# Two layers of graph attention on one core: value products of two units in one run, and four moves around it

## What is computed

```python
def layer0(x, adj):                       # x [128, 128, 256], adj [128, 128, 128]
    nx = ln(x) * g1 + b1
    q, k, v = heads(nx @ wq + bq), heads(nx @ wk + bk), heads(nx @ wv + bv)   # 8 heads of 32
    scores = q @ k.T / sqrt(32) + where(adj > 0, 0.1 * adj * adj, -inf)
    out = softmax(scores) @ v             # "value products"
    x1 = x + out @ wo + bo
    n2 = ln(x1) * g2 + b2
    return x1 + gelu(n2 @ w1 + b1) @ w2 + b2     # 256 -> 1024 -> 256
def layer1(x, adj):
    q, k, v = heads(x @ Wq + bq), heads(x @ Wk + bk), heads(x @ Wv + bv)
    scores = where(adj == 0, -inf, q @ k.T / sqrt(32))
    y = softmax(scores) @ v @ Wo + bo + x
    return ln(y) * gamma + beta
```

## Time and profile before

| | |
|---|---|
| median of 3 runs | 2196.47 us (2194.91 to 2199.86) |
| the profiled execution | 2196.19 us, span 2194.2 us |
| mean granted clock of TensorE | 0.989 |
| busy: PE, PEld | 98%, 85% |
| busy: DVE, ACT, POOL | 82%, 77%, 53% |
| DMA | 35 GB/s on the mean |

### The profile page before, as it was taken

How to read it: one execution, slowest core, us unless ns; L and a number is a source line. 1 busy time by engine, 2 the same in 40 slices (tenths; PEclk the granted TensorE clock), 3 DMA queues, 4 the chain that set the end, 5 groups by cost and what they waited for, 6 DMA issues and landing times.

```text
span 2194.2 us, 58906 instructions
## 1 busy us (share of the span) xinstructions
PE 2150.1 (98%) x20300; PEld 1859.1 (85%) x20300; DVE 1798.1 (82%) x8414; ACT 1682.3 (77%) x5646; POOL 1153.8 (53%) x1266
## 2 busy tenths in 40 slices
PE   7999999999999999999999999999999999999986
PEld 5788888888888888888888888888888888888875
DVE  6588888888888888888888888888888888888774
ACT  5578777778877778877787877787877787877773
POOL 4345655445655455555455555455555455554454
PEclk8899999999999999999999999999999999999998
DMA  4010111001111101111101111101110101110000
GB/s 128 25 32 31 40 33 36 27 29 37 37 35 31 32 28 37 34 39 31 32 26 40 33 40 30 30 28 40 33 40 27 33 28 40 33 40 26 26 14 17
DMA packets 94308, 75.74 MB, mean 35 GB/s; under 512 B 8128, under 2 KB 93760, under 8 KB 94016
## 3 DMA queue, kind: packets, MB, share of 16 engines
q1 hardware_dynamic: 94016, 71.99, 10.8%
HBM read 55.20 MB, written 16.78 MB: 33 GB/s over the span
## 4 chain that ended last, share of the span: by engine, by line
PE 96%; DVE 2%; issue 1%; ACT 1%; POOL 0%; DMA 0%; SPq 0%; POOLq 0%; ACTq 0%; DVEq 0%
PE p_bank L1132 67%; PE p_heads L1229 10%; PE p_heads L1216 8%; PE p_bank L1248 7%; PE p_bank L1151 4%; ACT scores L650 1%; DVE normed L885 0%; DVE probs_t L922 0%; DMA scores<-in_L_gnn_wk 0%; PE p_bank L1061 0%; PE p_bank L1087 0%; DVE scores L863 0%; ACT normed L661 0%; SPq L441 0%; DVE x_two L770 0%
## 5 line engine op out<-in xcount | busy, mean ns | idle before, releaser
L650 ACT ACTIVATE scores<-scores,negmax 128x128 f32<-128x128 f32 x2048 | 793.7, 392 | 22.5 <-DVE negmax L863 22.2
L584 POOL TENSOR_TENSOR scores<-scores,inverse 128x512 f32<-128x512 f32 x512 | 541.2, 1062 | 333.4 <-DVE inverse L874 333.4
L650 ACT ACTIVATION_READ_ACCUMULATOR scores<-scores,negmax 128x1 f32 x2048 | 391.9, 191 | 0.0
L1132 PEld LDWEIGHTS p_bank<-w_down,hidden 128*128 128x128 f32 x3072 | 374.7, 190 | 8.6 <-issue 5.9
L1132 PE MATMUL p_bank<-w_down,hidden 128*128 128x256 f32 x3072 | 381.9, 284 | 0.0
L1132 PE MATMUL p_bank<-normed,w_up 128*128 128x512 f32 x1536 | 370.5, 397 | 3.2 <-DVE normed L885 3.2
L1132 PEld LDWEIGHTS p_bank<-normed,w_up 128*128 128x128 f32 x1536 | 285.3, 189 | 68.9 <-issue 9.8
L1229 PE MATMUL p_heads<-ident,scores 128*128 128x128 f32 x2048 | 312.8, 276 | 9.2 <-issue 5.2
L863 DVE CUSTOM_DVE_ANT_0 scores<-p_heads,adj_a 128x128 f32<-128x128 f32 x1024 | 235.2, 286 | 44.4 <-issue 44.4
L673 ACT ACTIVATE p_bank<-p_bank,ready_cols 128x512 f32<-128x512 f32 x256 | 169.5, 662 | 132.8 <-PE p_bank L1132 127.1
L1229 PEld LDWEIGHTS p_heads<-ident,scores 128*128 128x128 f32 x2048 | 241.3, 141 | 35.3 <-DVE negmax L863 11.4
(11 more groups left out here) (117 smaller groups left out, 3698.0 us busy)
## 6 DMA issues: line engine op xcount, KB each, us to landing
res_a<-in_x SPq DMA_DIRECT2D x32, 512.0 KB, 3.8
out<-res_c SPq DMA_DIRECT2D x128, 128.0 KB, 1.7
x_in<-in_x SPq DMA_DIRECT2D x31, 512.0 KB, 3.8
adj_a<-in_adj SPq DMA_DIRECT2D x32, 256.0 KB, 2.9
adj_c<-in_adj SPq DMA_DIRECT2D x32, 256.0 KB, 2.8
piece_room<-in_L_gnn_w SPq DMA_DIRECT2D x2, 512.0 KB, 7.1
x_two<-in_x SPq DMA_DIRECT2D x1, 512.0 KB, 5.5
res_c<-in_L_gnn_w SPq DMA_DIRECT2D x1, 512.0 KB, 6.3
```

The source lines that it names most:

```text
L584: nc.gpsimd.tensor_tensor(rows_g, rows_g, inverse[:, step % 2, heads].unsqueeze(2).broadcast_to([P, HC, P]), ALU.mult).then_inc(probs_made, 1)
L650: last = nc.scalar.activation(scores[:, k % 2, h], scores[:, k % 2, h], ACT.Exp, scale=-1.0, bias=negmax[:, k % 2, h:h + 1], accum_out=tot ...
L1132: last = nc.tensor.matmul(dst, stationary(i), moving(j), start=(n == 0), stop=(n == total_n - 1))
```

## The change

Five things are changed.

1. The value products of two units stand in one run in steps 1, 3, 5 and 7, into one bank of 512 columns; `heads_high` and `heads_low` copy both units at once, and `probs_t` and `heads_t` have two rooms. The output products W stay one by one: the first of a pair in the step of the run, the second in the step after; in step 1 both. W of units C0 to C3 is thereby a step later than before, and so are their norm, `finish` and store. For stage M the norms of the last two units stand together in step 2.
2. Both V banks of stage A stand in the `early` place of step 2 (before: one `early`, one in `fill`).
3. On SP the load of `res_a` stands in front of store 1 instead of behind it.
4. On ACT the copies of a transposed block (`ahead`: XT M in step 2, XT N in step 7) stand in front of the second half of the exponentials, except in step 4.
5. At the start: bias products 7 and 2 are moved forward in pass 0; pieces 6 and 7 of the weights are split in steps 3 to 5 of pass 1 instead of 0 and 1; one `scaled_room` takes the place of two, with two more waits for it.

```diff
-HIGH_STEPS = {0: {1: [2], 4: [3], 5: [4], 6: [5]}, 1: {0: [6], 1: [7]}}
-LOW_STEPS = {0: {5: [3], 6: [4], 7: [5]}, 1: {0: [6], 1: [7]}}
+HIGH_STEPS = {0: {1: [2], 4: [3], 5: [4], 6: [5]}, 1: {3: [6, 7]}}
+LOW_STEPS = {0: {5: [3], 6: [4], 7: [5]}, 1: {4: [6], 5: [7]}}
...
+    by_step = {k: [] for k in steps}
     for r, k in enumerate(steps):
-        by_step[k] = ([("V", r - 2), ("W", r - 2)] if r >= 2 or pending else []) + (
-            [("T", r - 1)] if r >= 1 or pending else [])
+        by_step[k] += [("T", r - 1)] if r >= 1 or pending else []
+        by_step[k] += [("W", -3)] if r == 0 and pending else []
+        if r % 2 and (r >= 3 or pending):
+            by_step[k] += [("V", (r - 3, r - 2)), ("W", r - 3)]
+            if r == 1:
+                by_step[k] += [("W", r - 2)]
+            elif r < len(steps) - 1:
+                by_step[steps[r + 1]] += [("W", r - 2)]
     last = len(steps) - 1
-    tail = [("V", last - 1), ("T", last), ("W", last - 1), ("V", last), ("W", last)] if drain else []
+    tail = [("W", last - 2), ("V", (last - 1,)), ("T", last), ("W", last - 1), ("V", (last,)), ("W", last)] if drain else []
...
-        early = {1: ("Q", "A", 0), 2: ("V", "A", 0), 4: ("DOWN", 1), 6: ("Q", "C", 0), 7: ("V", "C", 0)}
+        early = {1: [("Q", "A", 0)], 2: [("V", "A", 0), ("V", "A", 1)], 4: [("DOWN", 1)], 6: [("Q", "C", 0)],
+                 7: [("V", "C", 0)]}
-        fill = {0: [("K", "A", 1)], 1: [("Q", "A", 1)], 2: [("V", "A", 1)],
+        fill = {0: [("K", "A", 1)], 1: [("Q", "A", 1)],
...
-            self.tail = self.tail[:-1] + [("V", "N", 0), self.tail[-1], ("V", "N", 1),
-                                          ("BIAS", 2), ("BIAS", 3), ("BIAS", 7)]
+            self.fill[7] = [("BIAS", 7)]
+            self.tail = self.tail[:1] + [("BIAS", 2)] + self.tail[1:-1] + [
+                ("V", "N", 0), self.tail[-1], ("V", "N", 1), ("BIAS", 3)]
...
-        probs_t = sb("probs_t", [P, H, P])
-        heads_t = sb("heads_t", [P, 2, KC, P], F32R)
+        probs_t = sb("probs_t", [P, 2, H, P])
+        heads_t = sb("heads_t", [P, 2, 2, KC, P], F32R)
-        scaled_rooms = [sb(f"scaled_room{i}", [P, 2, TOK]) for i in range(2)]
+        scaled_room = sb("scaled_room", [P, 2, TOK])
...
                 if s.c:
                     store(t, 0)
-                    store(t, 1)
                 if s.a and s.before is not None:
                     sp.wait_ge(*drained_use(t, ("DOWN", 1)))
                     sp.dma_start(res_a[:, :, :], x_view[:, bass.ds(t.group_a * GB, GB), :]).then_inc(res_a_loaded, 16)
                 if s.c:
+                    store(t, 1)
                     store(t, 2)
...
+                    for op in s.ahead.get(k, []) if not long else []:
+                        evacuate(t, op)
                     if k in s.units and k != s.behind and not long:
                         exps(t, k, 1)
-                    for op in s.ahead.get(k, []):
+                    for op in s.ahead.get(k, []) if long else []:
                         evacuate(t, op)
...
-                nc.scalar.activation(heads_t[:, HI].rearrange("p c n -> p (c n)"), p_bank[bank][:, 0:KC * P],
+                nc.scalar.activation(heads_part(HI, units), p_bank[bank][:, 0:len(units) * KC * P],
                                      ACT.Copy).then_inc(high_made, 1)
...
-                    if k == 2:
-                        for r in s.late.get(k, []):
-                            apply_norm(t, r, GB - 1)
+                    if k == 2 and s.m and s.pending:
+                        apply_norm(t, -1, 2)
+                        apply_norm(t, -1, 3)
...
+            def value_products(t, units):
+
+                bank, dst = take(t, ("O", units))
+                u_last, stage, _ = t.unit(units[-1])
+                pe.wait_ge(turned_out0, u_last + 1)
+                pe.wait_ge(turned_out1, u_last + 1)
...
+                for i, r in enumerate(units):
+                    _, _, b = t.unit(r)
+                    for h in range(H):
+
+                        j, c = h % HC, h // HC
+                        last = nc.tensor.matmul(dst[HD * j:HD * (j + 1), (i * KC + c) * P:(i * KC + c + 1) * P],
+                                                values[room(t, stage)][:, b, h * HD:(h + 1) * HD],
+                                                probs_t[:, parity(r), slot_of(c, j), :], start=True, stop=True)
+                last.then_inc(filled[bank], 1)
```

More of the change, by code:

```diff
@@ L88, in __init__ @@
         self.lag, self.tail = lags(self.steps, pending, drain)
-        self.late, waiting = {}, [-3] if pending else []
+        self.pending = pending
+        self.late, waiting = {}, []
         for k in self.steps:
@@ L137, in __init__, with use_units @@
         assert not self.looped or len(self.use) % BANKS == 0
+    def use_units(self, r):
+        return [use[1] for use in self.use if use[0] == "O" and use[1][0] == r]
     def number(self, ops):
@@ L330, in build @@
                                         piece_rooms[3][:, :, :])]
-        scaled = [as_piece(scaled_rooms[n % 2][:, :, :]) for n in range(8)]
+        scaled = [as_piece(scaled_room[:, :, :]) for n in range(8)]
         w1, w2 = w_view(L0 + "w1"), w_view(L0 + "w2")
@@ L410, in turned_columns, with parity, turned_rows, heads_part @@
             return p_heads[:, 2 * g:2 * g + 2, KC * P:2 * KC * P]
-        def turned_rows(g):
-            return probs_t[:, HC * g:HC * (g + 1)].rearrange("p (a h) n -> p a (h n)", a=2)
+        def parity(r):
+            return (r if r >= 0 else r + STEPS) % 2
+        def turned_rows(r, g):
+            return probs_t[:, parity(r), HC * g:HC * (g + 1)].rearrange("p (a h) n -> p a (h n)", a=2)
+        def heads_part(part, units):
+            first = parity(units[0])
+            return heads_t[:, part, first:first + len(units)].rearrange("p i c n -> p (i c n)")
         def room(t, what):
@@ L921, in turned, with heads_low @@
                 dve.wait_ge(probs_turned, u * KC + 2)
[L922 to L929, removed]
+                nc.vector.tensor_copy(turned_rows(r, 1), turned_columns(1)).then_inc(turned_out1, 1)
+            def heads_low(t, units):
+                bank, _ = t.bank(("O", units))
+                dve.wait_ge(high_made, t.high(("O", units)))
+                nc.vector.tensor_tensor(heads_part(LO, units), p_bank[bank][:, 0:len(units) * KC * P],
+                                        heads_part(HI, units).bitcast(F32), ALU.subtract).then_inc(drained[bank], 1)
             def add_residual(t, r):
@@ new lines, in project @@
+            def project(t, r):
+                for units in t.s.use_units(r):
+                    bank, number = t.bank(("O", units))
+                    pe.wait_ge(drained[bank], number)
+                bank, dst = take(t, ("W", r))
+                w = weight[weights_of[t.unit(r)[1]][3]]
+                three_passes(dst[:, 0:D], [(lambda i, c=c: heads_t[:, i, parity(r), c, :], lambda j, c=c: w[:, j, c, :])
+                                           for c in range(KC)]).then_inc(filled[bank], 1)
@@ L1235, in lagging @@
+            def lagging(t, op, which):
                 if op == "T":
                     for g in range(2):
-                        turn(t, r, g)
+                        turn(t, which, g)
                 if op == "V":
[L1239 to L1243, removed]
-                            pe.wait_ge(*drained_bank(*made(t, "V", stage, i)))
@@ L1245, in lagging @@
-                    for h in range(H):
-                        j, c = h % HC, h // HC
-                        last = nc.tensor.matmul(dst[HD * j:HD * (j + 1), c * P:(c + 1) * P],
-                                                values[room(t, stage)][:, b, h * HD:(h + 1) * HD], probs_t[:, slot_of(c, j), :],
-                                                start=True, stop=True)
-                    last.then_inc(filled[bank], 1)
-                if op == "W":
-                    bank, number = t.bank(("O", r))
-                    pe.wait_ge(drained[bank], number)
-                    bank, dst = take(t, ("W", r))
-                    w = weight[weights_of[stage][3]]
-                    three_passes(dst[:, 0:D], [(lambda i, c=c: heads_t[:, i, c, :], lambda j, c=c: w[:, j, c, :])
-                                               for c in range(KC)]
-                                 ).then_inc(filled[bank], 1)
+                    value_products(t, which)
```

28 lines of the change are left out of this document (14 added, 14 removed).

## The result

The changed kernel takes 2218.85 us (2217.77 to 2220.42), the kernel before 2196.47: ratio 1.0104, 95% interval 1.0093 to 1.0115. It is 1% slower, and the forecast of 2200 and its range up to 2217 were missed on the slow side. The profiled execution took 2218.9 us, span 2216.9, 22.7 more than the span before.

A forecast was written before the change was run, and what follows sets the result against it. PE's queue was taken to bound the loop. From 2196.2 us, 30 passes at +0.29 (+8.7), the start (-6.0) and the end (+1.5) gave 2200.4, forecast as 2200; own range 2190 to 2210, wider range 2178 to 2217.

The forecast's parts named there:

- wait in step 0: Step 0: PE waits for POOL's second probabilities behind finish of C3, biases, rstd and store; 0.64 us a pass.
- wait in step 6: Step 6, second transposes: PE comes 0.14 us earlier, POOL's row some 0.13 later; 0.15 us a pass (0 to 0.3).
- start, to pass 2: Passes 0 and 1: moved bias products and weight pieces gain 3.05, 1.3 and 2.7, less 1.0; net -6 us (-2 to -8).
- end, from pass 32 on: End: four units finished in one row instead of three, one finish (1.49) more; +1.5 us (0 to 4).
- V run: Value products of two units in one run on PE, four pairs a pass: saves 0.60 us a pass, 18 us in all.
- the 0.10 for the exponentials: Step 2: second exponentials come later behind the block's copies, delaying masks for step 3's transposes; 0.10 us a pass (0 to 0.25).
- 1 back: Pass 1: four weight copies ahead of step 4's exponentials, mostly under DOWN 1, and POOL's subtractions return 1 us of the start's gain.
- (b): Rival: DVE falls behind with doubled residuals, measurements and norms in steps 1 and 2, UP waits; 2215 to 2225 us, chance 0.14.
- upper bound in step 0: Step 0's stall at most 1.0 us a pass, if DVE's norm beside them stretches POOL's instructions.
- (a): Rival: POOL is not late, finish of C3 or its store ends sooner, PE keeps its gain; 2174 us (2168 to 2186), chance 0.18.
- (c): Rival: the wide copies end after W is due, each 0.1 us costing 0.4 a pass; 2212 us and up, chance 0.04.
- (d): Rival: the V run is not shorter, eight more products cost 0.57 us, stall about 0.75 a pass; 2214 us, chance 0.04.

The follow-up runs named there:

- e2: Changed kernel, with step 0's late probabilities on POOL ahead of store wait and res_c bias, and DVE's norm behind the copy of the turned probabilities: 2192.22 us, ratio 0.9983.
- f2: Changed kernel with e2, e4 and e7 together, and step 6's norm on DVE also behind its copy of the turned probabilities: 2178.42 us, ratio 0.9921.
- e6: Changed kernel, but ACT copies the blocks of steps 2 and 7 behind the second exponentials again, as before: 2235.26 us, ratio 1.0173.
- e3: Changed kernel, but C's finished blocks are written to and stored from a room of their own, so step 0's first res_c bias waits only for finish: 2211.53 us, 1.0066.
- e7: Changed kernel, but POOL's first res_a bias moves from step 5 into step 6, behind the probabilities of the second transposes: 2216.65 us, ratio 1.0088.
- e4: Changed kernel, but in pass 1 POOL scales weight piece 6 ahead of A's rstd in step 3 instead of behind it: 2215.81 us, ratio 1.0089.
- e9: Changed kernel without its start moves: bias products 2, 3, 7 at pass 0's end, weight pieces 6, 7 cut in steps 0, 1 of pass 1: 2222.98 us, 1.0122.
- e1: Changed kernel, but in step 0 POOL makes the late probabilities ahead of its wait for the store and the first res_c bias: 2238.85 us, ratio 1.0191.
- e8: Kernel before plus start moves alone: weight pieces 6, 7 cut in steps 3 to 5 of pass 1, bias products 7, 2 moved: 2199.84 us, ratio 1.0008.

## Why the prediction was wrong

The forecast by its terms, in us (left: as forecast; right: from the traces; the last two lines of the pass from e2 and f2):

```
                                   forecast   measured
pass with no wait, against before    -0.50      -0.49     (65.63 - 66.12; forecast: -0.60 + 0.10)
wait in step 0                       +0.64      +0.74     (5.97 - 5.23)
wait in step 6                       +0.15      +0.32     (5.54 - 5.22)
30 passes                            +8.7      +19.3      (30 x 0.57 = 17.1, late stores 2.2)
start, to pass 2                     -6.0       -3.05
end, from pass 32 on                 +1.5       +6.5
sum                                  +4.2      +22.7
```

The mechanism was right: the merged run pays on PE and POOL's row takes back more. The steps that failed are terms of the sum, each put too favourably. Of the 18.5 us between 4.2 and 22.7, the wait in step 6 has 5.1, the wait in step 0 3.0 and the late stores 2.2; the end has 5.0 and the start 3.0; the rest is rounding.

- **V run: right.** 1.01 us against 1.0; the steps without waits are 5.23 and 5.22 (forecast near 5.2) and 7.08 (near 7.1). That the whole line fits is partly luck: the 0.10 for the exponentials is not seen as such (the old order is worse, e6), steps 1 and 2 together came out 0.15 us longer than forecast, and step 5 0.14 shorter.
- **Step 0: the row was right, its spread was left out.** Counted from the start of step 7, the late probabilities were forecast to end at 10.9 us and end at 11.0. The forecast put the bias at the landing of the store, 0.07 us behind the rstd; e3 finds 0.15 us a pass for the store. But no room was left for stores that land later: the five late passes are 2.2 us.
- **Step 6: undersized by half.** I took PE to come 0.14 us earlier (+0.436 - 0.575). Step 5 grew by only 0.30, so PE came 0.27 earlier. And I looked at the transposes alone: DVE's copy behind them is next in line (e7, f2).
- **Start: "1 back" was 4.5.** Up to step 4 of pass 1 the -7.05 came (82.06 instead of 89.23 is 7.2). "1 back" for the copies in front of the exponentials was 3.6 in step 4 and 0.9 in step 5. I counted the four copies and hid them under DOWN 1; but they wait for POOL's scaling, which stands behind an rstd that DVE's sums for A release only when step 4 begins, and behind them the table load, the exponentials, their inverse, four norms, the mask and the addition for DOWN 1 follow one another through three engines. The 0.9 of step 5 goes with the clock: behind the wait of 3.53 us the granted clock is 0.50 from 92 to 96 us; in e4 and e9, without that wait, it is 1.00 in step 5, which takes 5.92 us.
- **The end: one row was carried over without its surroundings.** The finish of a fourth unit cost about what was forecast (2.0 us from the last scores on, against 1.5). What was left out is step 0 of pass 32, where the same POOL row waits 1.34 us for the store and PE stands 2.92 us. Behind it the granted clock is 0.58 and 0.50 in 2119 to 2122 and 2122 to 2126, and a V run takes 1.94 us instead of 1.08. The first three steps are 5.8 us longer than before; step 3 is 1.2 shorter. With the order of f2 pass 32 to the end is 99.2 us, +3.3; what makes up the rest was not tried.

Of the rivals, (b) names the time, 2215 to 2225, but not what happened: in the loop PE never waits for x_two; all three waits of that kind (5.9 us in sum) lie outside it. Its thought that DVE is close to the limit is right in another place, as e1 showed. The upper bound in step 0 had the pair of engines the wrong way round: it let DVE's norm stretch POOL's instructions, and it is POOL's that stretch the norm (last section). (a), (c) and (d) are out: POOL is late, heads_t is waited for only outside the loop (3.2 us in five waits), and the run is shorter. The residual's load ahead of a store and the single `scaled_room` were not tried alone; in the trace after no instruction waits for that load, as forecast.

## What to carry to other kernels

When an instruction moves into another step, write down the whole row of the engine that receives it, up to the next result that the bound engine needs, and then the same for the engine behind that: undoing the first link alone made this kernel slower (e1), both links made it faster than before (e2). A saving that is spread over a loop is kept only if the waits in it are moved with it: here a pass came out at +0.58 us, and with two reorders on POOL and two on DVE at -0.49. One-time work that is "hidden" must be followed back too: ask when its input is ready, not only what it runs under.

## What the runs showed of the hardware

**A norm on DVE that starts beside POOL waits for it.** The same form of instruction, 128x256 from SBUF to SBUF, lasts 0.40 to 0.41 us alone, but 1.36, 1.21 and 1.04 us in e1, e7 and e2, each time until 0.15 us after the end of a POOL bias (e1: 1060.01 and 1059.86; e7: 1038.46 and 1038.31). In the trace after, from 100 us on, all 180 norms that start while POOL works on an instruction of 256 or 512 columns end 0.15 to 0.28 us after it. A norm that starts 0.17 us ahead keeps its time (0.38 us at 1043.40), and POOL's probabilities beside it, at 1043.57, take 1.12 instead of 1.04. DVE's residual of the same size out of PSUM keeps its 0.41 to 0.43 inside a POOL bias. The Trainium skill, "SBUF — State Buffer", section "SBUF: two separate sides", says that a DVE instruction in a mode with two ports and a GpSimd instruction take one pair of ports as a lock, and the loser blocks; the traces agree, though no run shows in which mode the norm works. In the row that forecast e1 it would have been worth some 0.9 us a pass.

**Bias products in an idle stretch, and the clock.** Stretches at the end of pass 0 of the changed kernel, of before, of e8 and of e4 (length; busy time of PE, weight loads, DVE, ACT and POOL; the granted clock as a share of 2.4 GHz; DMA share and GB/s):

```profile
50.00:54.00 4.00, 3.67 (x53) 2.88 (x52) 2.48 (x9) 0.98 (x2) 2.31 (x4) 1.00 0.00 0
54.00:58.00 4.00, 4.00 (x38) 4.00 (x35) 3.01 (x13) 1.22 (x3) 0.93 (x2) 1.00 0.02 4
...
62.00:66.00 4.00, 3.39 (x8) 2.74 (x9) 1.07 (x2) 1.86 (x3) 0.45 (x1) 0.50 0.53 177
```

```profile
50.00:54.00 4.00, 1.88 (x11) 1.67 (x10) 0.40 (x1) 0.60 (x1) 2.38 (x3) 0.58 0.00 0
54.00:58.00 4.00, 4.00 (x32) 3.36 (x32) 2.87 (x10) 0.38 (x1) 0.55 (x1) 0.56 0.00 0
```

```profile
54.00:58.00 4.00, 4.00 (x25) 3.77 (x18) 1.13 (x7) 0.38 (x1) 0.55 (x1) 0.50 0.01 4
58.00:62.00 4.00, 4.00 (x20) 4.00 (x20) 1.08 (x5) 0.60 (x1) 0.00 (x0) 0.50 0.00 0
```

```profile
50.00:54.00 4.00, 3.84 (x31) 3.06 (x30) 2.27 (x7) 0.86 (x3) 0.76 (x2) 0.57 0.01 4
```

Before, PE was idle in much of 50 to 54 and the clock was at its lower level of 1.2 GHz for much of this stretch and the next; with bias product 2 in the gap it stayed at 2.4 through 58 and fell later (0.50 in 62 to 66). It stays at 2.4 from 46 to 58 in ten of the eleven traces with this order; in e4, with the same products in the gap, it fell all the same (0.57 in 50 to 54), so the products alone do not decide it. In e9, the changed kernel with these products back at the end, it is 0.71 in 50 to 54. In e8, where the product stands after the gap, its 16 records took 3.58 us instead of 1.84 (e8, then after):

```profile
54.23 3.58 PE L1061 MATMUL p_bank<-cols,res_c 128*128 128x1 f32 x16
```

```profile
48.73 1.84 PE L1084 MATMUL p_bank<-cols,res_c 128*128 128x1 f32 x16
```

Part of the 7.2 us at the start is thus the clock, which the forecast did not have; that the -7.05 came out right in sum is partly luck. How large that part is was not measured.
